# Attention with a gate, one core: the values' products of an even unit's four key blocks put into one run, and the table of times set anew

## The reference

```python
xn = layernorm(x)                                # x: 8 x 1024 x 512
q, k, v = xn Wq^T + bq, xn Wk^T + bk, xn Wv^T + bv    # 16 heads of 32
scores = q k^T / sqrt(32)
scores = where(i % 256 >= j % 256, scores, -1e30)     # i, j of 1024
attn = softmax(scores) v
s = attn Wo^T + bo
g = silu(clip((xn sign(Wf)^T) * scale + bias, -100, 100))
out = x + s * g
```

## Time and profile before

| what | value |
|---|---|
| median of 3 runs | 1672.88 us (1670.03 to 1674.52) |
| profiled execution | 1672.39 us |
| span of its instructions | 1670.6 us |
| PE busy | 1602.0 us, 96% |
| PEld, DVE, ACT, POOL busy | 685.3, 1184.2, 1195.6, 1239.8 us |
| granted PE clock, mean | 0.995 of 2.4 GHz |

### The profile page before, as it was taken

One profiled execution on the slowest core, in us unless ns is written; L12 is line 12 of the kernel. 1 busy time (PEld: TensorE's weight loads), 2 busy tenths in 40 slices (PEclk: granted clock), 3 DMA queues, 4 the chain that ended last, 5 costly groups with the idle time before them and its releaser, 6 DMA issues.

```text
span 1670.6 us, 34222 instructions
## 1 busy us (share of the span) xinstructions
PE 1602.0 (96%) x11931; PEld 685.3 (41%) x11931; DVE 1184.2 (71%) x1790; ACT 1195.6 (72%) x3057; POOL 1239.8 (74%) x1223
## 2 busy tenths in 40 slices
PE   9988999989999899998999999999999989999988
PEld 4333344434444344443444434443344434444433
DVE  7787776787667766686767866678676776667762
ACT  3476787777777777687776787866787777777762
POOL 0277767887788779887688776798768897678865
PEclk9999999999999999999999999999999999999999
DMA  7323312333224422243122532233312322222121
GB/s 214 118 36 74 89 41 64 96 85 76 52 65 98 91 56 52 79 112 79 46 58 71 126 70 49 61 86 101 86 41 63 99 77 63 52 58 71 44 66 51
DMA packets 182951, 125.97 MB, mean 75 GB/s; under 512 B 104734, under 2 KB 157214, under 8 KB 182332
## 3 DMA queue, kind: packets, MB, share of 16 engines
q1 hardware_dynamic: 182300, 123.40, 29.6%
q10 hardware_dynamic: 480, 0.39, 0.1%
HBM read 41.40 MB, written 17.02 MB: 35 GB/s over the span
## 4 chain that ended last, share of the span: by engine, by line
PE 77%; ACT 6%; issue 6%; POOL 4%; DVE 3%; SPq 3%; DMA 1%; POOLq 0%; ACTq 0%; DVEq 0%
PE pJ L576 30%; PE pO L820 13%; PE pJ L801 10%; PE pS L774 3%; PE pJ L797 3%; PE pJ L671 3%; PE pJ L675 3%; PE pJ L672 3%; POOL acc L1311 2%; SPq L1415 2%; PE pS L756 2%; PE pJ L740 2%; ACT pS L940 2%; ACT PT L920 2%; PE pS L757 1%
## 5 line engine op out<-in xcount | busy, mean ns | idle before, releaser
L1311 POOL TENSOR_TENSOR acc<-acc,PT 128x512 f32<-128x512 f32 (+1 forms) x714 | 874.7, 1262 | 15.8 <-PE pO L820 10.8
L920 ACT ACTIVATE PT<-pJ 128x512 f32<-128x512 f32 (+1 forms) x1080 | 614.7, 583 | 328.8 <-PE pJ L801 313.2
L801 PE MATMUL pJ<-QK 97*128 97x512 f16 (+3 forms) x1280 | 384.5, 318 | 5.5 <-ACT acc L920 3.4
L1172 DVE TENSOR_REDUCE mx<-pS 128x3 f32<-128x1536 f32 (+3 forms) x264 | 377.4, 1440 | 0.0
L1156 DVE TENSOR_REDUCE mx<-pS 128x1 f32<-128x384 f32 (+3 forms) x330 | 209.0, 636 | 139.9 <-PE pS L757 138.0
L1168 DVE TENSOR_REDUCE mx<-pJ 128x1 f32<-128x512 f32 (+3 forms) x264 | 151.7, 585 | 180.0 <-PE pJ L774 117.5
L820 PE MATMUL pO<-PT,V 128*32 128x512 f32 (+2 forms) x2800 | 259.4, 484 | 1.1 <-ACT PT L920 1.1
L940 ACT ACTIVATE pS<-pS,a 128x128 f32<-128x128 f32 (+1 forms) x480 | 251.3, 527 | 1.2
L797 PE MATMUL pJ<-QK 128*128 128x128 f16 x1024 | 180.6, 221 | 13.3 <-ACT PT L920 10.0
L576 PE MATMUL pJ<-xT,wh_k 128*128 128x512 f16 x512 | 192.5, 378 | 0.0
L576 PE MATMUL pJ<-wh_v,xT 128*128 128x512 f16 x512 | 189.9, 379 | 1.4 <-ACT acc L920 1.3
(11 more groups left out here) (177 smaller groups left out, 2681.8 us busy)
## 6 DMA issues: line engine op xcount, KB each, us to landing
QK<-sg SPq DMA_DIRECT2D x762, 64.0 KB, 2.0
xs<-in_x SPq DMA_DIRECT2D x60, 256.0 KB, 3.2
xr<-in_x SPq DMA_DIRECT2D x58, 256.0 KB, 3.1
out<-xr SPq DMA_DIRECT2D x58, 256.0 KB, 2.5
QK<-aT SPq DMA_DIRECT2D x256, 1.0 KB, 1.7
QK<-in_x SPq DMA_DIRECT2D x8, 256.0 KB, 4.0
rq<-moved SPq DMA_DIRECT2D x120, 2.0 KB, 1.8
QK<-in_mqk SPq DMA_DIRECT2D x2, 512.0 KB, 10.0
```

The lines of the kernel that those rows point to most:

```text
L801: ins = e.matmul(slot[:, to:to + 512 - q0], k4[0:97, j, kc], q4[0:97, j, q0:512], start=True, stop=True)
L920: e.activation(probabilities_at(i), bank("t", i)[:, 0:cols], ACT.Exp, scale=SS).then_inc(s_p, 1)
L1172: e.tensor_reduce(mx[:, par, part, :].rearrange("p (j q) -> p j q", q=4)[:, 0:3, qi], pS[:, :, c0:c0 + w], AX.X, ALU.max).then_inc(s_m0, 1)
L1311: e.tensor_tensor(a, a, PT[:, RING_AT[i] % NPT, 0:width * len(heads)].rearrange("p (j q) -> p j q", j=len(heads)), ALU.add).then_inc(s_ap, 1)
```

## The change

In an even unit the values' products of key blocks 0 to 3 are no longer two pairs (blocks 0 and 1 behind the tiles of block 1, blocks 2 and 3 behind those of block 3) but one run of four behind the last transposed tile. The pairs of odd units remain. The row sums of the odd unit before now take their time from this run (at_pv(n + 1, 0) plus TM["sm"][1]). All numbers of the table TM are new.

```diff
 TM = {
...
-    "pv": (1.15, 2.1, 0.32, 1.43, 1.47, 3.64),
+    "pv": ((0.81,), (0.32, 1.2, 1.49, 3.49)),
...
-    "qk": ((-18.77, -15.27, -2.04, 2.7), (-20.48, -15.72, -4.6, -1.86), (-15.89, -14.55, -5.64, 4.62), (-16.61, -13.39, -2.28, 5.09)),
+    "qk": ((-25.45, -14.82, -2.04, 4.1), (-20.64, -16.61, -4.24, 1.26), (-16.9, -16.78, -6.06, 2.91), (-16.75, -16.47, -2.28, 6.24)),
...
-    "sm": (2.88, -1.21, -0.25, 4.18),
+    "sm": (4.18, -0.21, 0.28, 2.97),
...
-    "c": ((0.77, 0.97), (-0.06, 1.16), (0.81, 0.94), (-1.08, 1.16)),
+    "c": ((1.06, 1.04), (0.23, 1.32), (1.25, 1.39), (-0.79, 1.32)),
...
+RUNS = ((0, 1, 2, 3),), ((0, 1), (2, 3), (4, 5), (6, 7))
+
+
+def run_of(n, kb):
+
+    return next((k, run) for k, run in enumerate(RUNS[n % NQS]) if kb in run)
+
+
 def at_pv(n, kb):
 
-    return at_t(T_LAST[n, kb | 1]) + TM["pv"][n % NQS * 2 + kb // 2] + 0.01 * (kb & 1)
+    k, run = run_of(n, kb)
+    return at_t(T_LAST[n, run[-1]]) + TM["pv"][n % NQS][k] + 0.005 * (kb - run[0])
+
+
+def at_direct(n, kb):
+
+    run = run_of(n, kb)[1]
+    return at_pv(n, run[0]) - 0.02 + 0.005 * (kb - run[0])
...
-    return at_pv(n, 3) + TM["sm"][0] if n % NQS == 0 else at_pv(n + 1, 1) + TM["sm"][1]
+    return at_pv(n, 3) + TM["sm"][0] if n % NQS == 0 else at_pv(n + 1, 0) + TM["sm"][1]
```

More of the change, by code:

```diff
@@ L39 @@
 TM = {
[L40 to L43 removed]
[12 rows of a table removed]
[L56 to L71 removed]
+    "s": ((22.32, 19.32, 17.99, 25.7, 31.12, 28.59, 35.69), (23.62, 19.45, 27.35, 17.65, 29.82, 32.46, 35.76), (25.75, 18.53, 23.01, 20.96, 35.92, 30.3, 34.49), (26.19, 19.05, 17.71, 22.57, 34.34, 36.66, 29.65)),
+    "s0": (18.79, 15.63, 24.32, 21.26, 29.88, 34.54, 37.34),
+    "e": ((-10.94, -7.75, -2.59), (13.24, 10.03, 12.3)),
+    "held": (1.06, -0.15, 1.33, 1.79, 1.62, 0.97, 1.68, 0.05),
[12 rows of a table added]
+    "gate": (-0.83, -1.29, 6.37, 4.32, 5.82),
+    "ln": ((-47.67, -23.43, -45.46, 36.11), (-79.34, 2.94, 0.28, 24.86), (-14.96, -1.17, -2.24, 7.46)),
+    "mx": (0.69, 0.13, -0.07),
+    "sh": (2.53, 1.97),
+    "c": ((1.06, 1.04), (0.23, 1.32), (1.25, 1.39), (-0.79, 1.32)),
+    "ex": (0.17, 1.13),
+    "mv": (2.16,),
+    "stage": (-0.74, 0.21),
+    "hl": (-6.41, -0.03),
+    "pr": (-0.09,),
+    "add": (2.95,),
+    "nrm": (-0.32, 0.76, 3.74, 3.24),
+    "out": (4.01, 3.65, 2.51),
+    "hi": ((7.03, 7.62), (4.95, 9.13)),
+    "vst": (0.41,),
+    "res": (0.53, 1.49),
 }
@@ L716, in direct_sums @@
                     for kb in DIRECT[n]:
-                        yield at_pv(n, kb & ~1) - 0.02 + 0.01 * (kb & 1)
+                        yield at_direct(n, kb)
                         first, last = T_FIRST[n, kb], T_LAST[n, kb]
```

26 lines of the change are left out of this document (4 added, 22 removed), and 18 rows, old and new, of the table TM.

## The result

The changed kernel takes 1678.23 us (median of 12 runs, 1674.65 to 1684.80), the kernel before, run beside it, 1674.32 us (12 runs, 1670.03 to 1675.48). The ratio is 1.0029, 95% interval [1.0015, 1.0043]: 0.3% slower, at the edge of what can be measured, where 10.6 us less were forecast. Its profiled execution took 1676.08 us, span 1674.2, mean clock 0.992 (before 1672.39, 1670.6 and 0.995).

What follows compares the result with a forecast made beforehand. PE was taken as the bound, busy 96% of the span. -7.8 (tiling) - 2.2 (end) - 1.9 (zrow) - 1.7 (odd units' start) + 3 (new waits) = -10.6 us against 1672.39 gives 1661.8 us; range 1651 to 1671.

Steps and rivals of the forecast that it cites:

- The changes of tiling, -7.8: PE's column-tile runs: 58 fewer changes by 0.095 us and 41 fewer runs by 0.055, together 7.8 us less.
- The end, -2.2: Last sums and products: 40 projection products now lie before the last projections, so PE's 2.2 us wait goes.
- The ring PT ... Nothing: PT holds 12 tiles, the even unit fills 11; its first slot is wanted five tiles after the run: no cost.
- The row sums ... POOL, which has to finish its additions first, gains time: Odd unit's row sums come some 3.6 steps later, giving POOL time; price 0, bounds -0.4 and +1 us.
- +3 for new waits: New table of times: 3 us of new waits set against 3.6 us of gains, since shifts move some from 0.
- zrow's: First row scores of groups 2, 14, 22, 26: transfers get 3.7 us more; half of 3.8 us waits goes, 1.9.
- L816's: Start of odd units: projections and row scores now separate their tiles; half of PE's 3.4 us ACT waits goes, 1.7.
- The bound of +12 us: Upper bound for all that the new table of times does; the lower was -15 us.
- A: Rival: drains go but waits fill what they leave; only the end and a little more is left, 1670 us; chance 0.15.
- B: Rival: the long run starves ACT, which then bounds each odd unit's start; 22.8 us more, 1684.6 us; chance 0.11.
- the prediction's own signs: Trace checks, among them: PE's waits sum to about 40 us or less; a steady batch element about a microsecond shorter.

Runs made afterwards that it cites:

- e12: The kernel before with only the changed kernel's eight times of the last output projections (o9): 1668.21 us, ratio 0.9973.
- e5: The changed kernel with unit 0's products alone in two pairs again: 1686.69 us, ratio 1.0085 to the kernel before.
- n2: The changed kernel with the last three POOL additions before every eighth unit's row sums cut to 8 columns of each head: 1670.66 us, ratio 0.9990.
- e2: The changed kernel with its new table, but the even units' products in two pairs again: 1685.64 us, ratio 1.0101 to the kernel before.
- e1: The kernel before with its old table, but even units' products merged into one run, row sums at their old place: 1691.73 us, ratio 1.0113.
- e3: The changed kernel with the odd unit's high and low parts (ACT, POOL) moved earlier, ahead of POOL's additions: 1685.66 us, ratio 1.0077 to the kernel before.
- e13: The changed kernel with unit 0's products in two pairs and untransposed scores of units up to 3 at their old times: 1675.60 us, ratio 1.0019.
- e15: The changed kernel with e13's mended start and POOL's 15 small Newton instructions one addition later, once in a batch element: 1679.54 us, ratio 1.0056.
- e11: The changed kernel with every eighth unit's row sums behind the merged run instead of directly before it: 1683.72 us, ratio 1.0069 to the kernel before.
- e17: The changed kernel with one POOL residual addition of each batch element moved behind the last five additions: 1688.67 us, ratio 1.0096 to the kernel before.

## Why the prediction was wrong

**The changes of tiling, -7.8: right.** 779 changes, 2.293 and 3.15 us, PE busy 3.5 us less in spite of a lower clock. With POOL's additions small, the tiles gain 1.44 us in each batch element over the same cut of the kernel before, where 7.8 / 8 is 1.0; what the other 0.4 comes from no run shows.

**The end, -2.2: right**, measured at 3.5 us alone (e12) and 4.3 in the changed kernel (7.9 us late at unit 63's first tile, 3.6 at the end of the span).

**"The ring PT ... Nothing", and what reads the first product: failed.** I went through pO and PT and did not ask who waits for the product of block 0. POOL's additions do, because they write the tile that it reads. In unit 0 that made the first row sums late by some 1.6 us (e5 against the changed kernel); the whole start, with the new times of the scores, costs about 5 us.

**"The row sums ... POOL, which has to finish its additions first, gains time": failed.** The order gave POOL 3.6 steps more and it still came later: the row sums of one unit in eight wait 1.17 us for it instead of 0.31. What n2 won by cutting POOL's last additions there, 6 to 7 us, is nearly the whole gain of the tiling. I had put bounds of -0.4 and +1 us on the sums. POOL also stands idle in new places: its waits on PE's products grew from 10.8 to 110.5 us.

```profile
L1326 POOL TENSOR_TENSOR acc<-acc,PT 128x512 f32<-128x512 f32 (+1 forms) x714 | 877.9, 1262 | 114.8 <-PE pO L835 110.5
```

That belongs to the new table, not to the merge (e2 has 112.5 us, e1 13.4), and it isn't what makes POOL late: in e3 it is 9.2 us, and the row sums still wait 5.9 us. e3's line of POOL and its wait of PE:

```profile
L1326 POOL TENSOR_TENSOR acc<-acc,PT 128x512 f32<-128x512 f32 (+1 forms) x714 | 878.1, 1264 | 13.6 <-PE pO L835 9.2
PE pJ L755 <- POOL acc L1326: 5.9, 5, 1.2
```

Which of POOL's moved instructions takes its reserve stays open.

**The other times: +3 for new waits was the term that was mis-sized.** Under the sum's other terms for waits PE's total would have gone down by 2.2 at the end, and by 1.5 and 1.6 as zrow's and L816's waits measured (forecast 1.9 and 1.7); it went up by 4.8. So the new waits are some 10 us where the prediction had put 3; the largest are 6.4 us more under L789 and 5.0 for POOL's additions. And the prediction held the clock at its upper level, where 10.4 us more at the lower one cost, as an estimate, 5 us. By the medians all other times together cost 15.2 us (3.9 + 7.8 + 3.5), where -1.9 - 1.7 + 3 is -0.6; e2 says nearly the same, 14.2 us (13.8 + 3.5 for its end, less 3.1 for its changes of tiling). Of zrow's four waits that were to go three went (groups 14, 22 and 26), but the first grew from 2.34 to 2.75 us and a new one of 1.26 us came at 567.8, so 6.4 of 7.9 us are left. The bound of +12 us would have held the 10 us of new waits, but not the clock's 5 with them. I had put it near the middle of two far ends with no row to stand on.

**The rivals.** A, waits fill what the drains leave, is what happened in the steady part, by POOL, which the prediction left out when it looked at the places of waiting. Two of the prediction's own signs say so: PE's eight largest waits alone sum to 51.5 us, not to 40, and a steady batch element is 0.24 us shorter, not about one. B, ACT starved at the start of odd units, did not: L816 waits for ACT 1.8 us in all, where 3.4 were before. That the time ended above A's 1670 is in the main the start's 5 us, as far as known.

What stays open: why e13 and e15, the same up to the place of 15 small POOL instructions in each batch element, part at unit 5; and what sends a subtraction into its long form. That POOL's additions stretch it fits place, order and the cut kernels (with small additions the pair at 375 us is gone, while the one at 342 us beside POOL's addition to Y stays at 2.37 us), but neither engine was run alone.

## What to carry to other kernels

Saved time on the bounding engine is paid out only if the engine that feeds the next rendezvous isn't later than it. After moving a run, list for every instruction in it who waits for its end, also those that wait in order to overwrite what it reads, and look for the smallest reserve. Price a new table of times by running it without the change it came with, and look which of that run's waits the full change doesn't have: here the table with pairs lay 13.8 us above the kernel before, and one line of it (the end) alone beat both kernels. Before a difference of a few us between two traces is given a cause, lay two executions of the same program side by side: here they differ by up to 3.7 us at one tile.

## What the runs showed of the hardware

**A DVE instruction can be held up by GpSimd for several of its instructions.** The subtraction takes 0.68 us beside small additions (median) and 0.94 beside whole ones; in the changed kernel's table two pairs of it take 2.37 us (beside POOL's addition to Y) and 2.31 us (beside the additions to acc) in each batch element, in the old table, where the median is 1.19, none takes over 1.78. Beside a run of additions a single one took 4.0 to 5.3 us in ten of the profiled executions, through three to four whole additions. Where it starts does not decide: 0.32 to 0.33 us ahead of the run, four took 5.3 us and 13 took 0.9. In the long form of 5.3 us POOL's additions take 1.00 (384 columns) and 1.27 us (512 columns) each, the medians of the kernel before, and the one subtraction lasts through four of them; in the short form the addition of 384 columns takes 1.44 us.

**That makes a kernel's runs scatter.** Four profiled executions ran the same instructions up to 374 us, the changed kernel's, e11's, n2's and e17's. The changed kernel's has no subtraction over 1.78 us and is 7.2 us late at unit 12; the others have one of 4.04, 3.63 and 3.73 us at 175 us and are 10.9, 10.0 and 10.4 late. Of the 16 subtractions of 4.0 us and more, 15 have a stretch of the lower clock close behind them; in e15 they start at 572.5, 777.8, 982.6, 1187.5 and 1393.4 us and the clock falls at 581.8, 786.6, 991.4, 1196.2 and 1401.0. The changed kernel's runs span 10 us and e15's 23, the kernel before's 5.5. In the changed kernel the run at a mean clock of 0.994 took 1674.65 us and the one at 0.988 took 1684.80; that long subtractions made its long runs fits this, but those runs have no trace. In n2, after a wait of 2.04 us for ACT at 181 us, the stretches (span, then PE, PEld, DVE, ACT and POOL busy, the clock third from the end) read:

```profile
175.00:180.00 5.00, 3.87 (x26) 1.89 (x24) 5.00 (x3) 2.81 (x11) 4.22 (x4) 1.00 0.10 21
180.00:185.00 5.00, 3.24 (x18) 0.92 (x18) 2.86 (x5) 4.59 (x14) 0.00 (x0) 0.73 0.80 189
185.00:190.00 5.00, 5.00 (x49) 2.08 (x46) 3.38 (x8) 3.34 (x11) 1.27 (x1) 0.93 0.29 71
```

From unit 4's third block to unit 5's this run fell back by 6.2 us (3.5 to 9.7 late). So a single profile of such a kernel must be read with its run's time beside the median: the changed kernel's profiled run, 1676.08 us, had no long subtraction, and its median is 2.2 us above it.
